# The order of value matmuls and row transposes in a fused attention loop

## The chip, the cores and the metric

One core of a Trainium2 chip. The metric is the device time of one execution in microseconds. The kernel before takes 1733.1 us (median of 3 executions, 1732.15 to 1733.57).

## What is computed

Four layers follow each other on x, 2048 tokens of width 256; each adds a layer-normed result to x. The change concerns the first alone, latent attention:

```
n   = layernorm(x)
cq  = rms_norm(n @ w_qa.T)            # 192 wide
q   = (cq @ w_qb.T), 16 heads of 128 + 64 (the 64 with rotary positions)
ckv = n @ w_kva.T                     # 64 latent + 64 rotary
scores = q k^T * scale, causal; attn = softmax(scores)
out = attn @ v, all heads, @ w_o.T
x   = x + layernorm(out)
```

A mixture of experts, a gated linear recurrence and a quantized feed-forward layer follow. Each of them starts from layernorm(x) and is not touched.

## The kernel before

The kernel runs in stages; each is a block in which the five engines work through queues of their own, tied by semaphores. The first stage (to about 100 us) makes the latents and folds the weights. The second, 100 to 1271 us, is the attention loop in which the change lies. The others (1275 us to the end) do the three later layers.

**Work of the loop.** The 16 tiles of 128 query rows are taken in pairs, a long one and a short one: 15 and 0, 14 and 1, and so on (`tiles_in_order`, L469). A group is 4 heads of one tile, and groups alternate between the long tile and the short one: group 0 is tile 15, group 1 is tile 0, group 2 is tile 15 again; 8 groups to a pair, 64 in all. For each head the key columns up to the diagonal are cut into chunks of up to 4 blocks of 128 keys (`chunk`, L475): 4 chunks a head for tiles 15 to 12 (groups 0 to 31, the long ones), 1 chunk a head for tiles 0 to 3; 3 and 2 chunks in groups 32 to 63. There are 640 chunks. A chunk of n blocks costs n transposes and 3n value matmuls.

**Steps.** TensorE's steps are `project` (the group's queries, L576), `turn` (transposes them, L583, after POOL's rotary steps, L763 to L770, semaphore `roped`), `scores` (L597 to L602), `probs` (transposes the exponentials of a chunk, L615), `values` (L657 to L659, three matmuls a block: the split of the transposed probabilities in `pT_hi` and `pT_lo` times the latents), `o_turn` (L623, transposes normalised head results), `sum` (L641, output projection over all heads of a tile, 24 matmuls) and `x_turn` (L630, transposes the normed rows of the tile for the next layer).

**Transpose banks.** `probs`, `o_turn` and `x_turn` take turns on two PSUM banks, `pT[0]` and `pT[1]`, in the order of the plan (`t_index`, L545). Before the n-th of them TensorE waits in `bank_t` (L604) until ScalarE has copied the one two before it out (L697 `pT_hi`, L702, L706) and VectorE has subtracted (L818 `pT_lo`, L822, L826 `lT_lo`):

```
if n >= 2:
    pe.wait_ge(sem("t_hi"), n - 1)
    pe.wait_ge(sem("t_lo"), n - 1)
return pT[n % 2]
```

**Values and the group's end.** All 4 heads of a group gather in the one bank `pO`. After the last values of a group VectorE takes the reciprocal of the row sums (L834) and writes `O` (L836, `o_out`); the first values of the next group wait for that (L651):

```
if c == 0 and p % HG == 0 and p:
    pe.wait_ge(sem("o_out"), p // HG)
```

In VectorE's queue `o_out` stands at the step of the group's last values, and the `pT_lo` of the probs step just before it comes right behind (L873 to L879).

**The plan.** One list of steps, written by a planner (L481 to L542), sets the order on all engines. Scores of a chunk are appended, and after them, by a small table (L529), `one_behind()` is called 0 to 3 times: it appends `probs(at)`, then `values(at - 2)` (LAG is 2), and then counts down the steps in `later` (`pass_steps`). `later` holds, among others, what follows a tile's sum: `y_measure` after 2 calls, `y_add` after 4, `x_measure` after 5, `x_norm` after 7 and `x_turn` after 8 (L515). `x_norm` (ScalarE, L719) writes `xn` when POOL has the deviation (L141, L143, L777); `x_turn` transposes it; `x_turn` number u belongs to the u-th tile in order. Sixteen of these exist; the last two lie behind the last values. `turn` of a group is planned at the second head of the group before it, and `sum` at the third head of a group. In the plan before, `x_turn` 0, 2 and 4 stand one scores step ahead of a `turn`, with two more calls and then a `sum` behind it; 6, 8, 10 and 12 likewise, with the 3- and 2-chunk tiles; 1, 3 and 5 stand right before the boundary from a short tile into a long one; 7, 9, 11 and 13 stand two scores ahead of the probs of the next long group.

Of the kernel before, what the change touches and what calls it, by code (L numbers as in the profile page):

```python
# [41 lines left out]
HG = 4  # L42
# [32 lines left out]
def build(nc, x, w_lat, w_qn, w_qpe, w_kn, w_v, w_o, q_ln, kv_ln, cos2, sin2, gw, wg, wu, wd, sel,  # L75
          l_in, l_gate, l_b, l_lam, qg, qu, qd, sg, su, sd, out):
    with ExitStack() as whole:
# [89 lines left out]
        with ExitStack() as att:  # L167
# [279 lines left out]
            with ExitStack() as loop:  # L447
# [27 lines left out]
                chunk = [(p, c, min(4, tile_at(p) + 1 - 4 * c)) for p in range(NP) for c in range(tile_at(p) // 4 + 1)]  # L475
                first = [next(n for n, k in enumerate(chunk) if k[0] == p) for p in range(NP)] + [len(chunk)]
                n_chunks = first[NP]
                LAG = 2


                plan = [("project", 0), ("turn", 0), ("project", 1)] + [("scores", k) for k in range(first[1])]  # L481
# [3 lines left out]
                def pass_steps():  # L485
                    for entry in list(later):
                        entry[0] -= 1
                        if entry[0] <= 0:
                            plan.append(entry[1])
                            later.remove(entry)  # L490

                def one_behind():
                    at = state["behind"]
                    plan.append(("probs", at))
                    if at >= LAG:
                        values_planned(at - LAG)
                    state["behind"] += 1
                    pass_steps()

                def values_planned(at):  # L500
                    plan.append(("values", at))
                    p = chunk[at][0]
                    if at + 1 != first[p + 1] or p % HG != HG - 1:
                        return
                    u, g = groups[p // HG]
                    if g == 1:
                        later.append([2, ("o_turn", (u, 0))])
                    if g == 3:
                        later.append([2, ("o_turn", (u, 1))])
                        sums_due.append(u)  # L510

                def sum_heads():
                    u = sums_due.pop(0)
                    plan.append(("sum", u))
                    for delay, step in ((2, "y_measure"), (4, "y_add"), (5, "x_measure"), (7, "x_norm"), (8, "x_turn")):  # L515
                        later.append([delay, (step, u)])

                state = {"behind": 0}
                for p in range(1, NP):
                    n = first[p + 1] - first[p]  # L520
                    placed = False
                    for k in range(n):
                        if k == 0 and p % HG == 2 and sums_due and ("o_turn", (sums_due[0], 1)) in plan:
                            sum_heads()
                        plan.append(("scores", first[p] + k))
                        last = k == n - 1
                        if k == 0 and p % HG == 1 and p // HG + 1 < NG:
                            plan.append(("turn", p // HG + 1))
                        for _ in range({4: (1, 0, 0, 3), 3: (1, 0, 2), 2: (0, 2), 1: (1,)}[n][k]):  # L529
                            one_behind()  # L530
                            if last and not placed:
                                placed = True
                                if p % HG == 3 and p // HG + 2 < NG:
                                    plan.append(("project", p // HG + 2))
                while state["behind"] < n_chunks:
                    one_behind()
                for k in range(LAG):
                    values_planned(n_chunks - LAG + k)
                while later or sums_due:
                    if sums_due and ("o_turn", (sums_due[0], 1)) in plan:  # L540
                        sum_heads()
                    pass_steps()  # L542
# [541 lines left out]
        with ExitStack() as banks:  # L1084
# [70 lines left out]
            plan = [("up", 0), ("up", 1), ("gate", 0), ("split", 0), ("gate", 1)] + [step for slot in slots for step in slot]  # L1155
# [458 lines left out]
```

## Time and profile before

| | |
|---|---|
| median of 3 executions | 1733.1 us |
| the profiled execution | 1734.25 us, its span 1732.5 us |
| mean granted TensorE clock | 0.976 of full speed |
| TensorE matmul busy | 1568.3 us (91% of the span) |
| TensorE weight loads | 1322.7 us (76%) |
| VectorE busy | 1207.4 us (70%) |
| ScalarE busy | 1021.0 us (59%) |
| POOL busy | 301.2 us (17%) |

How to read it: the span is from the first to the last instruction of the profiled execution; the time holds some 1.8 us around it. Busy shares are of the whole span. Matmuls overlap on the array, so two rows that start 0.03 us apart can each be 0.19 us long: for TensorE the distance from start to start tells what a step costs. "Idle before" is the time that an engine did nothing before an instruction, and the name behind the arrow is what ended it.

### The profile page before, as it was taken

The numbers are of one execution on the slowest core, as the hardware profiler recorded it, in microseconds if no ns is written. First come the engines' busy times: TensorE is split into PE (matmuls) and PEld (weight loads), VectorE is DVE, ScalarE is ACT, GpSimd is POOL, SyncE is SP. The second block draws the span as 40 slices with busy tenths as digits, with TensorE's granted clock in tenths as the row PEclk, the third lists the DMA queues.
The fourth block names the chain that finished last, engine by engine and source line by source line (L and its number), as shares of the span: only waits on it lengthen the run. The fifth ranks groups of instructions, "written<-read, shape, count | busy, mean of one in ns | idle before, by whom it ended". The sixth has DMA issues, their size and how long they took to land. (4 is left out here: it accounts for less than half of the span.)

```text
span 1732.5 us, 38201 instructions
## 1 busy us (share of the span) xinstructions
PE 1568.3 (91%) x14452; PEld 1322.7 (76%) x14452; DVE 1207.4 (70%) x2600; ACT 1021.0 (59%) x2017; POOL 301.2 (17%) x743
## 2 busy tenths in 40 slices
PE   3679999999899999999999999999938999988997
PEld 1357787788788778888888888888836878866886
DVE  3847776777777677778777878787855547566564
ACT  2336665666576566667667667667624355555573
POOL 3511111211111211211121121121010012020231
PEclk9879999999999999999999999999978999999999
DMA  8000000000000000000000000000012200000000
GB/s 240 1 0 2 2 1 2 2 2 2 2 1 2 2 1 2 2 2 2 2 2 2 2 2 2 2 2 2 2 40 65 57 1 1 1 28 13 1 25 25
DMA packets 27814, 23.54 MB, mean 14 GB/s; under 512 B 9692, under 2 KB 25180, under 8 KB 27508
## 3 DMA queue, kind: packets, MB, share of 16 engines
q1 hardware_dynamic: 22324, 14.77, 3.1%
q10 hardware_dynamic: 5312, 6.33, 1.2%
q8 instruction: 120, 1.97, 0.5%
q14 instruction: 58, 0.48, 0.1%
HBM read 19.00 MB, written 2.10 MB: 12 GB/s over the span
## 5 line engine op out<-in xcount | busy, mean ns | idle before, releaser
L697 ACT ACTIVATE pT_hi<-pT 128x512 f16<-128x512 f32 (+3 forms) x640 | 341.2, 533 | 304.5 <-PE pT L615 303.0
L818 DVE TENSOR_TENSOR pT_lo<-pT,pT_hi 128x512 f16<-128x512 f32 (+3 forms) x640 | 387.4, 607 | 149.0 <-ACT pT_hi L697 141.9
L686 ACT ACTIVATE pr<-pS,nmx 128x512 f32<-128x512 f32 (+3 forms) x640 | 400.4, 626 | 26.1 <-DVE nmx L809 24.6
L806 DVE TENSOR_REDUCE cmx<-pS 128x1 f32<-128x512 f32 x576 | 338.7, 616 | 65.3 <-PE pS L602 59.9
L615 PE MATMUL pT<-ident,pr 128*128 128x128 f32 x2176 | 347.8, 276 | 16.4 <-DVE pT_lo L818 14.8
L615 PEld LDWEIGHTS pT<-ident,pr 128*128 128x128 f32 x2176 | 252.3, 140 | 48.6 <-ACT pr L686 24.7
L657 PE MATMUL pO<-c_hi,pT_hi 128*128 128x65 f16 x2176 | 265.6, 194 | 18.4 <-DVE O L836 17.7
L597 PE MATMUL pS<-lT_hi,qT_hi 128*128 128x512 f32 (+2 forms) x640 | 265.8, 415 | 3.0 <-ACT pr L686 3.0
L658 PE MATMUL pO<-c_lo,pT_hi 128*128 128x65 f16 x2176 | 266.4, 193 | 0.0
L659 PE MATMUL pO<-c_hi,pT_lo 128*128 128x65 f16 x2176 | 263.7, 192 | 0.0
L602 PE MATMUL pS<-lT_hi,qT_lo 128*128 128x512 f32 (+2 forms) x640 | 256.3, 400 | 0.0
L598 PE MATMUL pS<-lT_lo,qT_hi 128*128 128x512 f32 (+2 forms) x640 | 234.9, 367 | 0.0
L1221 PE MATMUL pGU<-lT_hi,W_all 128*128 128x512 f32 (+1 forms) x640 | 220.4, 403 | 16.0 <-ACT sgb L1301 12.1
L657 PEld LDWEIGHTS pO<-c_hi,pT_hi 128*128 128x128 f16 x2176 | 205.9, 97 | 28.4 <-ACT pT_hi L697 20.5
L658 PEld LDWEIGHTS pO<-c_lo,pT_hi 128*128 128x128 f16 x2176 | 204.1, 98 | 6.6
L659 PEld LDWEIGHTS pO<-c_hi,pT_lo 128*128 128x128 f16 x2176 | 205.2, 97 | 0.0
L1221 PEld LDWEIGHTS pGU<-lT_hi,W_all 128*128 128x128 f32 (+1 forms) x640 | 121.2, 189 | 47.3 <-ACT sgb L1301 16.3
L763 POOL TENSOR_TENSOR qt<-qs,sn 128x128 f32<-128x128 f32 x64 | 29.2, 456 | 704.6 <-ACT qs L674 704.6
L602 PEld LDWEIGHTS pS<-lT_hi,qT_lo 128*128 128x128 f32 x640 | 124.1, 194 | 16.8
L597 PEld LDWEIGHTS pS<-lT_hi,qT_hi 128*128 128x128 f32 x640 | 120.8, 189 | 16.9 <-ACT pr L686 3.0
L598 PEld LDWEIGHTS pS<-lT_lo,qT_hi 128*128 128x128 f32 x640 | 122.1, 191 | 11.2
L1221 PE MATMUL pGU<-lT_lo,W_all 128*128 128x512 f32 (+1 forms) x320 | 127.2, 398 | 0.0
(243 smaller groups left out, 2507.3 us busy)
## 6 DMA issues: line engine op xcount, KB each, us to landing
X<-in_x SPq DMA_DIRECT2D x4, 512.0 KB, 6.9
wo<-in_w_o ACTq DMA_DIRECT2D x1, 2048.0 KB, 14.1
out<-X SPq DMA_DIRECT2D x8, 256.0 KB, 2.0
raw<-in_wd SPq DMA_DIRECT2D x14, 128.0 KB, 2.1
raw<-in_wg SPq DMA_DIRECT2D x13, 128.0 KB, 2.8
raw<-in_wu SPq DMA_DIRECT2D x13, 128.0 KB, 2.7
wqn<-in_w_qn ACTq DMA_DIRECT2D x1, 1536.0 KB, 17.8
raw<-in_qg SPq DMA_DIRECT2D x6, 128.0 KB, 2.5
```

Source lines behind the costliest of these rows:

```text
L597: pe.matmul(o, q_hi, lT_hi[:, 2, ks], start=True, stop=False)
L598: pe.matmul(o, q_hi, lT_lo[:, 2, ks], start=False, stop=False)
L602: pe.matmul(o, q_lo, lT_hi[:, 2, ks], start=False, stop=True).then_inc(sem("scored"), 1)
L615: m = pe.transpose(o[:, k * P:(k + 1) * P], pr[:, at % RING, k * P:(k + 1) * P], ident[:])
L657: pe.matmul(o, hi, c_hi[:, j, 0:KVL + 1], start=(j == 0), stop=False)
L658: pe.matmul(o, hi, c_lo[:, j, 0:KVL + 1], start=False, stop=False)
L659: m = pe.matmul(o, lo, c_hi[:, j, 0:KVL + 1], start=False, stop=(j == tile_at(p)))
L686: act.activation(pr[:, at % RING, 0:n * P], pS[at % 4][:, 0:n * P], ACT.Exp, bias=nmx[:, p % 4:p % 4 + 1]).then_inc(sem("exped"), 1)
L697: act.activation(pT_hi[:, a % 4, 0:chunk[a][2] * P], src, ACT.Copy).then_inc(sem("t_hi"), 1)
L806: ch.inc(dve.tensor_reduce(cmx[:, p % 2, c:c + 1], pS[at % 4][:, 0:n * P], AX.X, ALU.max))
L818: dve.tensor_tensor(pT_lo[:, a % 4, 0:w], src, pT_hi[:, a % 4, 0:w], ALU.subtract).then_inc(sem("t_lo"), 1)
L1221: mm = pe.matmul(pGU[bank % 3][0:r, :], W_all[:, m, 2 * g + i, k * P:k * P + r], xT[j][:, k, ts], start=(q == 0), stop=(q == 5))
```

## The change

In `one_behind`, values are no longer planned at once but put in `values_due`. If the first one due is the first chunk of a group, and no `scores` step stands in the plan since the values before it, it is held until the next call, and then both are planned, behind the next `probs`. All other values are planned in the same call as before. At the end of the plan what is still due comes before the last two. Beside that, `x_turn` comes 10 calls after its sum in place of 8. The instructions of each step and their waits stay as they are; the waits count in the new order.

```diff
--- before.py
+++ after.py
@@ -493,7 +493,13 @@
                     at = state["behind"]
                     plan.append(("probs", at))
                     if at >= LAG:
-                        values_planned(at - LAG)
+                        values_due.append(at - LAG)
+                    new_group = values_due and chunk[values_due[0]][1] == 0 and chunk[values_due[0]][0] % HG == 0
+                    done = ("values", values_due[0] - 1) if values_due else None
+                    drained = not new_group or done not in plan or any(k[0] == "scores" for k in plan[plan.index(done):])
+                    if drained or len(values_due) > 1:
+                        while values_due:
+                            values_planned(values_due.pop(0))
                     state["behind"] += 1
                     pass_steps()
 
@@ -512,10 +518,11 @@
                 def sum_heads():
                     u = sums_due.pop(0)
                     plan.append(("sum", u))
-                    for delay, step in ((2, "y_measure"), (4, "y_add"), (5, "x_measure"), (7, "x_norm"), (8, "x_turn")):
+                    for delay, step in ((2, "y_measure"), (4, "y_add"), (5, "x_measure"), (7, "x_norm"), (10, "x_turn")):
                         later.append([delay, (step, u)])
 
                 state = {"behind": 0}
+                values_due = []
                 for p in range(1, NP):
                     n = first[p + 1] - first[p]
                     placed = False
@@ -534,8 +541,8 @@
                                     plan.append(("project", p // HG + 2))
                 while state["behind"] < n_chunks:
                     one_behind()
-                for k in range(LAG):
-                    values_planned(n_chunks - LAG + k)
+                for at in values_due + list(range(n_chunks - LAG, n_chunks)):
+                    values_planned(at)
                 while later or sums_due:
                     if sums_due and ("o_turn", (sums_due[0], 1)) in plan:
                         sum_heads()
```

## Rows read from the trace of the kernel before

**Rows 1.** Window 100 to 1275 us: length, busy by engine, clock, DMA share, GB/s

```profile
100.00:1275.00 1175.00, 1101.54 (x12017) 953.87 (x12016) 879.05 (x1813) 754.65 (x1490) 200.95 (x484) 0.99 0.01 2
```

**Rows 2.** Groups by line, TensorE: count, busy, mean ns, idle before, releasers

```profile
L615 PE MATMUL pT<-ident,pr 128*128 128x128 f32 x2176 | 347.8, 276 | 16.4 <-DVE pT_lo L818 14.8 <-ACT pr L686 0.4
...
L657 PE MATMUL pO<-c_hi,pT_hi 128*128 128x65 f16 x2176 | 265.6, 194 | 18.4 <-DVE O L836 17.7 <-DVE pT_lo L818 0.5
...
L630 PE MATMUL pT<-ident,xn 128*128 128x128 f32 x32 | 7.3, 314 | 15.4 <-ACT xn L719 13.8 <-ACT pT_hi L697 1.0 <-DVE pT_lo L818 0.6
```

**Rows 3.** Timeline, boundary into group 14: start, length, engine, line [idle before]

```profile
384.82 0.42 DVE L836 TENSOR_TENSOR O<-pO,rl 128x256 f32<-128x256 f32 x1
385.16 0.68 DVE L818 TENSOR_TENSOR pT_lo<-pT,pT_hi 128x512 f16<-128x512 f32 x1
...
385.39 0.19 PE L657 MATMUL pO<-c_hi,pT_hi 128*128 128x65 f16 x1 [0.65 <-DVE O L836]
...
385.66 0.19 PE L657 MATMUL pO<-c_hi,pT_hi 128*128 128x65 f16 x1
...
385.99 0.30 PE L615 MATMUL pT<-ident,pr 128*128 128x128 f32 x1
```

**Rows 4.** Timeline, boundary into group 10, TensorE

```profile
315.72 0.63 PE L615 MATMUL pT<-ident,pr 128*128 128x128 f32 x4 [1.47 <-DVE pT_lo L818]
316.19 0.19 PE L657 MATMUL pO<-c_hi,pT_hi 128*128 128x65 f16 x1
```

**Rows 5.** Timeline, x_turn 0 and the turns after x_turn 0 and 4

```profile
292.21 0.44 PE L630 MATMUL pT<-ident,xn 128*128 128x128 f32 x2 [0.91 <-ACT xn L719]
292.41 0.37 PE L597 MATMUL pS<-lT_hi,qT_hi 128*128 128x256 f32 x1
...
294.67 0.49 PE L583 MATMUL pQ<-ident,qs 128*128 128x128 f32 x3
...
292.99 0.45 POOL L770 TENSOR_TENSOR qs<-qs,qt 128x128 f32<-128x128 f32 x1
...
585.89 0.46 POOL L770 TENSOR_TENSOR qs<-qs,qt 128x128 f32<-128x128 f32 x1
...
587.92 0.60 PE L583 MATMUL pQ<-ident,qs 128*128 128x128 f32 x4
```

**Rows 6.** Timeline, after x_turn 6 and x_turn 12: POOL, TensorE, VectorE

```profile
731.30 0.46 POOL L770 TENSOR_TENSOR qs<-qs,qt 128x128 f32<-128x128 f32 x1
...
731.93 0.61 PE L583 MATMUL pQ<-ident,qs 128*128 128x128 f32 x4
...
734.49 0.36 PE L641 MATMUL pQ<-Wvo_hi,OT_hi 128*128 128x256 f32 x1
...
734.20 0.68 DVE L818 TENSOR_TENSOR pT_lo<-pT,pT_hi 128x512 f16<-128x512 f32 x1
...
1141.64 0.36 PE L641 MATMUL pQ<-Wvo_hi,OT_hi 128*128 128x256 f32 x1
...
1142.01 0.68 DVE L818 TENSOR_TENSOR pT_lo<-pT,pT_hi 128x512 f16<-128x512 f32 x1
```

**Rows 7.** Timeline, around x_turn 9, TensorE then VectorE

```profile
889.21 0.44 PE L630 MATMUL pT<-ident,xn 128*128 128x128 f32 x2 [1.26 <-ACT xn L719]
...
891.68 0.63 PE L615 MATMUL pT<-ident,pr 128*128 128x128 f32 x4
...
892.33 0.47 PE L597 MATMUL pS<-lT_hi,qT_hi 128*128 128x512 f32 x1
...
893.12 0.52 PE L615 MATMUL pT<-ident,pr 128*128 128x128 f32 x3
...
892.29 0.68 DVE L818 TENSOR_TENSOR pT_lo<-pT,pT_hi 128x512 f16<-128x512 f32 x1
...
893.62 0.69 DVE L818 TENSOR_TENSOR pT_lo<-pT,pT_hi 128x512 f16<-128x512 f32 x1
```

**Rows 8.** Timeline, the tail, TensorE

```profile
1267.66 0.69 PE L630 MATMUL pT<-ident,xn 128*128 128x128 f32 x2 [4.33 <-ACT xn L719]
```

## Prediction

> **What bounds the kernel now.** I read the busy times by window first. In the attention loop (100 to 1275 us) TensorE is busy 94% of the time with its clock at 0.99 of full speed, VectorE 75%, ScalarE 64% [rows 1]. TensorE works through its queue in order, so a wait that it removes is time won, and work pushed out of a wait is time lost, unless another wait swallows it. The groups by line show where it idles: 16.4 us before the transposes of the probabilities (14.8 of them until a `pT_lo`), 18.4 us before the values (17.7 until `O`), 15.4 us before the transposes of the normed rows (13.8 until `xn`) [rows 2]. The change aims at the last two. The most that it can win is therefore about 17.7 plus 15.4 less what the tail keeps: `x_turn` 14 alone waits 4.33 us for its rows, with nothing left to put in front of it [rows 8].
>
> **Part one, the first values of a group.** I replayed the planner: 31 of the 63 group boundaries have no scores between the old group's last values and the new group's first, all those in the 4-chunk/1-chunk half (tiles 15 to 12 beside tiles 0 to 3); boundaries in the other half are unchanged. No instruction is added or removed. Call the new group's first chunk d. The order was probs(d+1), values(d-1), probs(d+2), values(d), probs(d+3), values(d+1); it becomes probs(d+1), values(d-1), probs(d+2), probs(d+3), values(d), values(d+1).
>
> What then waits? probs(d+3) writes the transpose bank of probs(d+1), so it waits for `pT_lo`(d+1). VectorE's queue runs `O` of the old group first and that `pT_lo` right behind it. At the boundary into group 14 `O` ends at 385.24 and `pT_lo` at 385.84; the values start at 385.39, 0.15 after `O`, and probs(d+3) at 385.99, 0.15 after `pT_lo` [rows 3]. So the old order already ran probs(d+3) at the first moment its bank was free, and the values lay hidden between two waits that VectorE sets. The new order waits for the later of the two (385.99, as before) and then still has the values to do. Nothing is won; each boundary loses the issue time of values(d). Four blocks of three matmuls start 385.39, 385.66 (the fourth): 0.27 over nine matmuls, 31 ns each, 0.092 us a block [rows 3].
>
> By blocks: the 16 entries into a small tile have 1, 2, 3 or 4 blocks, four entries each, 40 blocks, 3.7 us. The 15 entries into a wide tile have 4 blocks; three of them are in part two, the other 12 give 48 blocks, 4.4 us. Sum 8.1 us. What swallows some: between a small entry and the wide one about 6 us later VectorE is nearly saturated, and where the y and x steps also lie there (three times, 9 blocks, 0.8 us) its own queue sets the next boundary. I take 1.0 off: **plus 7.1**. Bounds: half of it, 3.6, if VectorE swallows the small entries and more; 9 if the switch between kinds of matmul also costs. Below zero is excluded by the pinned bank.
>
> The 31 ns can be set against a rule. "TensorE: Matmul & The Clock Gate", section Back-to-back issue gap, of the Trainium skill gives 81 ns for a pair of weight load and matmul of 128 columns in a real stream; by that figure, as an estimate, the 264 matmuls would cost 21 us. The rows decide here.
>
> **Part two, the normed rows.** `x_turn` moves two probs steps later. It issues two transposes (0.20 us of TensorE: 292.21 to the next at 292.41 [rows 5]), one copy on ScalarE and one subtract on VectorE; no DMA is concerned, POOL's order stays. It uses a transpose bank too, so moving it changes which bank every step between gets. Four kinds of place:
>
> (a) x_turn 0, 2, 4. TensorE idles 0.91 at the first [rows 5]. Once that is gone, the `turn` behind it becomes late: it needs POOL's rope, which ends at 293.44 for a turn at 294.67, and at 586.35 for one at 587.92 [rows 5]; a turn that waits for it starts about 0.15 after (731.76 to 731.93 is the nearest row [rows 6]). So 1.08, 1.08 (the middle one has the same distance as the first) and 1.42 are won. The moved `x_turn` lands ahead of a sum that waits for `qT_lo` anyway. **Minus 3.5.** Bounds 3.0 and 3.9.
>
> (b) x_turn 1, 3, 5, just ahead of a wide entry. It took the bank of probs(d+2), which therefore stood 1.47 us behind `pT_lo` [rows 4]. Now probs(d+2) runs before the wait (0.47 saved, 315.72 to 316.19) and `x_turn` (0.20) after it; values(d) are no longer in a gap but were not before either. **Minus 0.7** for three; 0.5 to 0.9.
>
> (c) x_turn 6, 8, 10, 12. The turn behind it starts 0.17 after the rope [rows 6], so the turn cannot move, and nothing is won. The transposes now come right before the head sum, two banks behind a probs whose `pT_lo` is late: for 6 it ends at 734.88, for 12 at 1142.69, while the sums began at 734.49 and 1141.64 [rows 6]. The sum needs no transpose bank; `x_turn` does. With 0.15 and its own 0.20 the sums start at 735.23 and 1143.04: 0.74 and 1.40 lost; by the same steps 1.07 and 1.22 for 8 and 10. The sum takes 3 us and drains every queue, so this is kept. **Plus 4.4.** Bounds 3.0 (the `pT_lo` comes earlier because `lT_lo` has left its front) and 5.5.
>
> (d) x_turn 7, 9, 11, 13. Taking 9: its 1.26 us go, but probs 421 waits for a `pT_lo` that is tied to `qT_lo`, so TensorE is only 0.83 ahead. `x_turn` then waits for the `pT_lo` of 892.29 to 892.97, 0.41 earlier without the subtract: it starts at 892.70, the scores behind it at 892.90 where they were at 892.33. The transposes at 893.12 then fall into the other bank and need the `pT_lo` of 893.62 to 894.31, less 0.4, behind `O`: 894.05 [rows 7]. With the values, which waited a little before, 0.8 us is lost. The others, whose rows repeat the pattern, give 0.75, 0.6 and 0.5. **Plus 2.6.** Bounds 1.0 and 3.5.
>
> The tail: x_turn 14 now follows the 15th's norm on ScalarE, which waits for its own deviation anyhow; zero.
>
> **Sum.** 7.1 - 3.5 - 0.7 + 4.4 + 2.6 = plus 9.9 us. The profiled execution took 1734.25 (span 1732.5), 1.15 over the median of 1733.1; it would become 1744.2, the median 1743.0. About 0.2% (3.5 us) is what a measurement can tell from no change.
>
> **The rivals.**
> - *Faster.* The moved rows keep all that their stalls cost outside the tail (15.4 less the 4.33 of x_turn 14 and somewhat for the last one, about 10.5), and the displaced values vanish in the next wait. That needs ScalarE and VectorE to run (c) and (d) early enough that the bank is free when `x_turn` comes, 0.75 to 1.4 us earlier than rows 6 show. Point of decision: whether the sum starts before its `pT_lo` plus 0.35. For it: the stalls are real, VectorE is 25% idle. Against: the `pT_lo` hang on the pinned `turn`. 1733.1 - 10.5 = 1722.6, some 1723. Chance 0.08.
> - *No change to be seen.* Half of the values' cost swallowed (3.6), (c) and (d) at their low bounds (4.0), (a) and (b) as above (-4.2): plus 3.4, 1736.5; a little less is 1735. Chance 0.14, with the case that few boundaries are really deferred (then part two alone, plus 2.8).
> - *Slower still.* The copies of the moved rows, now among the densest copies of (d), delay `O` and all behind it, and the switch costs: 9 - 3.5 - 0.5 + 5.5 + 3.5 + some 3 = plus 17, 1750. Chance 0.13.
> - *Forecast.* 1743, own range 1737 to 1748. Chance 0.65.
>
> The range 1736 to 1748 takes the forecast's bounds (3.6 - 3.9 - 0.9 + 3.0 + 1.0 = 2.8 at the lowest, 9 - 3.0 - 0.5 + 5.5 + 3.5 = 14.5 at the highest) and leaves the faster case and most of the slowest outside. Chances: faster 0.08, within 0.2% 0.14, slower 0.78.
>
> **What would show it.** In the profile after: the idle time before the values until `O` is near 0, and about as much and more (some 35 to 40 us: the 16.4, the 17.7 and part of the values' 8.1) stands before the transposes of the probabilities until `pT_lo`; probs(d+3) starts 0.15 after it. The idle time before `x_turn` until `xn` keeps only the tail's; some 2 to 4 us until `pT_lo` take its place. Turns 10, 18 and 26 start 0.15 after the rope. The span from 100 to 715 us grows by about 3, from 715 to 1275 by about 7. The prediction is wrong if probs(d+3) starts without a wait, if the sums 7 to 13 start no later against their turns than now, or if the loop's first half gets shorter.

## The result, and the profile after

The changed kernel takes 1742.56 us (median of 5, 1740.94 to 1747.11) against 1733.1 (median of 5, 1731.09 to 1735.1): plus 9.5 us, a ratio of 1.006 with a 95% interval of 1.005 to 1.0071. The forecast was 1743.0. The profiled execution is the slowest of the five, 1747.11 with a span of 1745.4; what is known of the 4.6 us between it and the median is told at the end. The lines of the code after L518 are 7 higher than before (L615 is now L622, L657 is L664, L630 is L637, L818 is L825, L836 is L843).

First TensorE's groups by line in the changed kernel, with the columns of [rows 2]:

```profile
L622 PE MATMUL pT<-ident,pr 128*128 128x128 f32 x2176 | 347.7, 276 | 32.3 <-ACT pT_hi L704 16.7 <-DVE pT_lo L825 13.7 <-ACT lT_hi L713 0.9
...
L664 PE MATMUL pO<-c_hi,pT_hi 128*128 128x65 f16 x2176 | 262.6, 194 | 0.6 <-DVE pT_lo L825 0.5
...
L590 PE MATMUL pQ<-ident,qs 128*128 128x128 f32 x256 | 39.7, 279 | 7.6 <-POOL qs L777 7.0
...
L630 PE MATMUL pT<-ident,O 128*128 128x128 f32 x128 | 20.1, 280 | 17.6 <-ACT pT_hi L704 15.0 <-DVE pT_lo L825 2.4
L637 PE MATMUL pT<-ident,xn 128*128 128x128 f32 x32 | 7.1, 307 | 11.9 <-DVE pT_lo L825 6.3 <-ACT xn L726 5.2 <-ACT pT_hi L704 0.4
```

Two of these groups in the kernel before, which [rows 2] leave out:

```profile
L583 PE MATMUL pQ<-ident,qs 128*128 128x128 f32 x256 | 39.7, 278 | 4.2 <-POOL qs L770 3.6
...
L623 PE MATMUL pT<-ident,O 128*128 128x128 f32 x128 | 20.1, 280 | 1.4 <-DVE pT_lo L818 0.5
```

The 17.7 us that the values waited for `O` are gone, as the change wants it. They stand elsewhere: the transposes of the probabilities idle 32.3 us where it was 16.4, and the transposes of the heads (`o_turn`, L630, the old L623) idle 17.6 us where it was 1.4. The normed rows' 13.8 us until `xn` have shrunk to 5.2, the tail's alone, but 6.3 us until `pT_lo` stand there now where it was 0.6; and the turns wait 7.0 us for POOL's rope where it was 3.6. The work is the same; the waits have moved and TensorE's order behind them is worse.

Why `o_turn`: replayed, the plan has one between probs(d+2) and probs(d+3) at 15 of the 31 boundaries, those behind the second and the fourth group of a tile. There `o_turn` takes the bank of probs(d+1) and is the step that waits for `pT_lo`(d+1); probs(d+3) follows it, and the held values come behind both. The price is that of the other boundaries, as e1 shows.

The boundary into group 14 again, VectorE, ScalarE, TensorE, to be held against [rows 3]:

```profile
385.98 0.42 DVE L843 TENSOR_TENSOR O<-pO,rl 128x256 f32<-128x256 f32 x1
386.33 1.47 DVE L825 TENSOR_TENSOR pT_lo<-pT,pT_hi 128x512 f16<-128x512 f32 x2
...
385.27 0.60 ACT L704 ACTIVATE pT_hi<-pT 128x512 f16<-128x512 f32 x1 [1.63 <-PE pT L622]
...
387.15 0.52 PE L622 MATMUL pT<-ident,pr 128*128 128x128 f32 x3 [1.26 <-ACT pT_hi L704]
387.51 0.19 PE L664 MATMUL pO<-c_hi,pT_hi 128*128 128x65 f16 x1
...
388.24 0.48 PE L604 MATMUL pS<-lT_hi,qT_hi 128*128 128x512 f32 x1
```

From the start of `O` to the transposes behind it were 385.99 - 384.82 = 1.17 us before and are 387.15 - 385.98 = 1.17 now. TensorE then does the first two chunks of values together, 387.51 to 388.24. The releaser column names ScalarE's `pT_hi`; the one that this bank needs had ended at 385.87. The first of the two subtracts of the L825 row is the one that the step needs: it ends at 387.01 (its length in the kernel before was 0.68), 0.14 ahead of the transposes. Experiment e6 shows it.

Around x_turn 0, to be held against [rows 5]:

```profile
294.58 0.45 POOL L777 TENSOR_TENSOR qs<-qs,qt 128x128 f32<-128x128 f32 x1
...
295.18 0.63 PE L590 MATMUL pQ<-ident,qs 128*128 128x128 f32 x4
...
296.36 0.41 PE L637 MATMUL pT<-ident,xn 128*128 128x128 f32 x2
```

The turn starts 0.15 after the rope's end (295.03); it was 1.23. `x_turn` stands behind it, without a wait. Turn 18 starts 0.15 after the rope too, turn 26 0.24 after it: there the scores ahead of the turn end no sooner, and the rope is not the limit.

Ahead of sums 7 and 13, to be held against [rows 6]:

```profile
735.42 0.63 PE L590 MATMUL pQ<-ident,qs 128*128 128x128 f32 x4 [0.74 <-POOL qs L777]
...
738.54 0.41 PE L637 MATMUL pT<-ident,xn 128*128 128x128 f32 x2 [0.37 <-ACT pT_hi L704]
738.77 0.36 PE L648 MATMUL pQ<-Wvo_hi,OT_hi 128*128 128x256 f32 x1
...
737.71 0.68 DVE L825 TENSOR_TENSOR pT_lo<-pT,pT_hi 128x512 f16<-128x512 f32 x1
...
1151.61 0.41 PE L637 MATMUL pT<-ident,xn 128*128 128x128 f32 x2 [1.01 <-DVE pT_lo L825]
1151.88 0.35 PE L648 MATMUL pQ<-Wvo_hi,OT_hi 128*128 128x256 f32 x1
```

From turn 34 to sum 7 were 734.49 - 731.93 = 2.56 us and are 3.35; the turn itself, with the stall ahead of it gone, waits 0.74 us for the rope. `x_turn` starts 0.15 after the end of `pT_lo` (738.39).

Around x_turn 9, to be held against [rows 7]:

```profile
897.96 0.68 DVE L825 TENSOR_TENSOR pT_lo<-pT,pT_hi 128x512 f16<-128x512 f32 x1
...
899.29 0.69 DVE L825 TENSOR_TENSOR pT_lo<-pT,pT_hi 128x512 f16<-128x512 f32 x1
...
898.79 0.41 PE L637 MATMUL pT<-ident,xn 128*128 128x128 f32 x2 [1.04 <-DVE pT_lo L825]
898.96 0.48 PE L604 MATMUL pS<-lT_hi,qT_hi 128*128 128x512 f32 x1
900.12 0.52 PE L622 MATMUL pT<-ident,pr 128*128 128x128 f32 x3 [0.22 <-ACT lT_hi L713]
```

This is the chain of part (d): `x_turn` behind one `pT_lo`, and the next transposes in the other bank, behind the next `pT_lo` (899.98), 0.14 after it.

**Place by place.** The plan has the same turns and sums in every kernel here, so the timeline gives for each of them by how much it starts later than in the kernel before. What the difference grows by between two of them is what the place between them cost. This table is worked out so, in us, from one profile of each kernel; its first row is how far a kernel is ahead where the loop begins, before anything of its edit:

```
                           forecast       after                e2 (turns alone)
start of the loop             -           -0.57                -4.14 (clock)
held values, all 31          +7.1         +8.4                  -
x_turn 0, 2, 4      (a)      -3.5         -1.06 -1.05 -1.29    -1.04 -1.02 -1.30
x_turn 1, 3, 5      (b)      -0.7         -0.27 -0.30 -0.33    -0.50 -0.49 -0.43
x_turn 6, 8, 10, 12 (c)      +4.4         +0.79 1.10 1.27 1.47 +0.79 1.10 1.27 1.46
x_turn 7, 9, 11, 13 (d)      +2.6         +0.71 0.76 0.61 0.24 +0.71 0.76 0.61 0.25
the loop                     +9.9         +11.0                +2.5
```

### The profile page after: what moved, and what is told of

It reads as the page before. It is cut to its first block and busy times, and to the rows that moved or that the text cites. A ratio compares the mean times of both kernels' runs of the same rounds, so it can differ in the third digit from the quotient of the medians.

```text
span 1745.4 us, 38201 instructions
## 1 busy us (share of the span) xinstructions
PE 1569.1 (90%) x14452; PEld 1322.4 (76%) x14452; DVE 1210.2 (69%) x2600; ACT 1022.2 (59%) x2017; POOL 301.5 (17%) x743
## 5 line engine op out<-in xcount | busy, mean ns | idle before, releaser
L825 DVE TENSOR_TENSOR pT_lo<-pT,pT_hi 128x512 f16<-128x512 f32 (+3 forms) x640 | 387.8, 607 | 146.2 <-ACT pT_hi L704 139.2
L622 PE MATMUL pT<-ident,pr 128*128 128x128 f32 x2176 | 347.7, 276 | 32.3 <-ACT pT_hi L704 16.7
L622 PEld LDWEIGHTS pT<-ident,pr 128*128 128x128 f32 x2176 | 252.4, 140 | 66.8 <-ACT pr L693 43.2
L664 PE MATMUL pO<-c_hi,pT_hi 128*128 128x65 f16 x2176 | 262.6, 194 | 0.6 <-DVE pT_lo L825 0.5
L664 PEld LDWEIGHTS pO<-c_hi,pT_hi 128*128 128x128 f16 x2176 | 205.8, 97 | 4.1 <-ACT pT_hi L704 0.9
L1228 PEld LDWEIGHTS pGU<-lT_hi,W_all 128*128 128x128 f32 (+1 forms) x640 | 121.2, 189 | 47.5 <-ACT sgb L1308 16.4
## 6 DMA issues: line engine op xcount, KB each, us to landing
wo<-in_w_o ACTq DMA_DIRECT2D x1, 2048.0 KB, 13.8
wqn<-in_w_qn ACTq DMA_DIRECT2D x1, 1536.0 KB, 17.7
```

Source lines behind the costliest of these rows:

```text
L622: m = pe.transpose(o[:, k * P:(k + 1) * P], pr[:, at % RING, k * P:(k + 1) * P], ident[:])
L664: pe.matmul(o, hi, c_hi[:, j, 0:KVL + 1], start=(j == 0), stop=False)
L825: dve.tensor_tensor(pT_lo[:, a % 4, 0:w], src, pT_hi[:, a % 4, 0:w], ALU.subtract).then_inc(sem("t_lo"), 1)
L1228: mm = pe.matmul(pGU[bank % 3][0:r, :], W_all[:, m, 2 * g + i, k * P:k * P + r], xT[j][:, k, ts], start=(q == 0), stop=(q == 5))
```

## The experiments

Medians and ratios are against the kernel before, run on the same chip (medians there 1732.0 to 1733.2).

**e1, the held values alone.** The change with its other part undone:

```diff
-                    for delay, step in ((2, "y_measure"), (4, "y_add"), (5, "x_measure"), (7, "x_norm"), (10, "x_turn")):
+                    for delay, step in ((2, "y_measure"), (4, "y_add"), (5, "x_measure"), (7, "x_norm"), (8, "x_turn")):
```

> Only the values part of the change; x_turn stays at 8 steps. Theory (the transposes behind the held values wait for the same pT_lo as before, so the values' issue time is laid bare): 0.37 us at each wide entry, 0.1 to 0.37 at each small one, except at the three boundaries with an x_turn ahead of them, where less; the loop 8 to 9 us longer, 1741 to 1742 us. The idle time before the values until O goes to near 0 and comes back before the transposes. Rival one (the wait is filled, the loss of the whole change is all in the moved x_turn): 1733 or less. Rival two (half is swallowed by VectorE between a small and a wide entry): plus 4 to 5, 1737.5.

Measured: 1740.79 us, ratio 1.005 (1.0036 to 1.0064). The turns put the loop at plus 8.4. The groups by line:

```profile
L622 PE MATMUL pT<-ident,pr 128*128 128x128 f32 x2176 | 347.2, 276 | 30.6 <-DVE pT_lo L825 16.8 <-ACT pT_hi L704 12.7 <-ACT pr L693 0.4
...
L664 PE MATMUL pO<-c_hi,pT_hi 128*128 128x65 f16 x2176 | 262.9, 194 | 0.6 <-DVE pT_lo L825 0.5
```

By place: a wide entry costs 0.36 to 0.41 us (one 0.26), a small one 0.13, 0.19, 0.29 and 0.37 for tiles 0, 1, 2 and 3, so 0.13 for the first block and some 0.08 for each further one; the three wide entries behind an `x_turn` cost 0.00. Entries with an `o_turn` between the two probs cost the same as those without: tile 0 costs 0.12 to 0.13 at both kinds. Both rivals fall: the wait is not filled, and nothing is swallowed between a small and a wide entry.

**e2, the moved x_turn alone.** The kernel before with (10, "x_turn").

> Only x_turn at 10 steps; the values are not held. Theory (each place has its own sign): minus 1.1 to 1.4 us at x_turn 0, 2 and 4; minus 0.3 to 0.7 at 1, 3 and 5; plus 0.8 to 1.5 at 6, 8, 10, 12 just ahead of the sum; plus 0.2 to 0.8 at 7, 9, 11, 13; together plus 1 to 3, 1734 to 1736 us. Rival (the move is a plain gain of its 10 us of stalls, and the loss of the whole change lies in the values alone): 1723 us, and e1 at 1750.

Measured: 1735.86 us, ratio 1.0018 (1.001 to 1.0027); the loop plus 2.5, as in the table. The stalls before `x_turn` did shrink:

```profile
L630 PE MATMUL pT<-ident,xn 128*128 128x128 f32 x32 | 7.1, 307 | 12.0 <-DVE pT_lo L818 6.3 <-ACT xn L719 5.2 <-ACT pT_hi L697 0.4
```

8.6 us of the 13.8 until `xn` are gone, 5.7 of them are back until `pT_lo`, so that the group idles 12.0 us where it was 15.4; and the kernel is slower. The plain-gain rival falls. e1 and e2 add up to the whole change: 8.4 + 2.5 = 10.9 against 11.0 in the loop. At one kind of place they do not: x_turn 1, 3 and 5 win 1.42 us here and 0.90 in the whole change. With `x_turn` out of the way the values have their gap ahead of `O` back (0.66 us of idle time before them at the boundary into group 10 in e2), and holding them lays them bare again; in e1, with `x_turn` still there, it cost nothing.

**e6, held values and pT_lo ahead of O.** e1, and in VectorE's queue, at the first 31 boundaries:

```diff
                             elif step == "values" and at + 1 in first and chunk[at][0] % HG == HG - 1:
+                                if turned is not None and at < 316:
+                                    t_lo(turned)
+                                    turned = None
                                 o_out(chunk[at][0] // HG)
```

> As e1, and at the first 31 boundaries VectorE makes pT_lo ahead of O. Theory (the transposes wait for pT_lo, not for pT_hi as the releaser column says): they start about 0.45 us earlier at a wide entry and 0.2 to 0.4 at a small one, and the values behind them then wait for O, which is later by the pT_lo; the wait is partly filled at last: 0.25 us won at a wide entry, 0.1 at a small one, against e1 minus 4 to 6, some 1737 us. Rival (the transposes wait for ScalarE's pT_hi): they start where they do in e1, O is later by up to 0.6 us, and the time is e1's or more, 1742 to 1750.

Measured: 1741.31 us, ratio 1.0045 (1.0032 to 1.0058). The boundary into group 2, first in e1 and then in e6:

```profile
165.35 0.42 DVE L843 TENSOR_TENSOR O<-pO,rl 128x256 f32<-128x256 f32 x1
165.69 0.68 DVE L825 TENSOR_TENSOR pT_lo<-pT,pT_hi 128x512 f16<-128x512 f32 x1
...
164.61 0.60 ACT L704 ACTIVATE pT_hi<-pT 128x512 f16<-128x512 f32 x1 [1.62 <-PE pT L622]
165.85 0.59 ACT L704 ACTIVATE pT_hi<-pT 128x512 f16<-128x512 f32 x1
...
166.52 0.63 PE L622 MATMUL pT<-ident,pr 128*128 128x128 f32 x4 [1.39 <-ACT pT_hi L704]
166.98 0.19 PE L664 MATMUL pO<-c_hi,pT_hi 128*128 128x65 f16 x1
```

```profile
165.17 0.69 DVE L825 TENSOR_TENSOR pT_lo<-pT,pT_hi 128x512 f16<-128x512 f32 x1
165.98 0.42 DVE L843 TENSOR_TENSOR O<-pO,rl 128x256 f32<-128x256 f32 x1
...
164.53 0.60 ACT L704 ACTIVATE pT_hi<-pT 128x512 f16<-128x512 f32 x1 [1.62 <-PE pT L622]
165.78 0.59 ACT L704 ACTIVATE pT_hi<-pT 128x512 f16<-128x512 f32 x1
...
166.00 0.63 PE L622 MATMUL pT<-ident,pr 128*128 128x128 f32 x4 [0.95 <-ACT pr L693]
166.55 0.19 PE L664 MATMUL pO<-c_hi,pT_hi 128*128 128x65 f16 x1
```

ScalarE's rows are the same to 0.08, `pT_lo` ends 0.51 earlier, and the transposes start 0.52 earlier, 0.14 to 0.15 after it in both: they wait for `pT_lo`, whatever the releaser column names. At this place all that e1 lost is won back (plus 0.02 against the kernel before). Over all boundaries it is 1.0 us in the loop (plus 7.4 against 8.4), not the 4 to 6 that I wrote: at 15 of the 31 boundaries an `o_turn` stands between the two probs, and that needs the `O` which now comes later (its idle time is 18.9 us, 16.7 of it until `O`); and with tiles 2 and 3 the values wait for `O` too. The medians (1741.31 and 1740.79) are too coarse to show it. The mechanism holds, the size was missed.

```profile
L630 PE MATMUL pT<-ident,O 128*128 128x128 f32 x128 | 20.5, 283 | 18.9 <-DVE O L843 16.7 <-ACT pT_hi L704 1.4 <-DVE pT_lo L825 0.5
```

**e7, the same swap in the kernel before.**

> The kernel before, with VectorE's pT_lo ahead of O at the first 31 boundaries; nothing else. Theory: the first values of a group wait 0.2 (tile 0) to 0.6 us longer for O and the transposes behind them come later by the same less what they waited for pT_lo: plus 0.45 to 0.5 at a wide entry, 0.15 to 0.5 at a small one, plus 8 to 13, 1741 to 1746 us. Rival (the order of the two on VectorE does not matter): 1733.

Measured: 1743.07 us, ratio 1.0059 (1.0046 to 1.0071); the loop plus 9.9. The values wait 37.1 us where it was 18.4:

```profile
L657 PE MATMUL pO<-c_hi,pT_hi 128*128 128x65 f16 x2176 | 265.9, 194 | 37.1 <-DVE O L836 27.6 <-ACT pT_hi L697 8.9 <-DVE pT_lo L818 0.5
```

The rival falls. So at a boundary VectorE's two outputs are the bound, and TensorE's order fits VectorE's only if what waits for the first of them comes first.

**e3, x_turn 0 to 5 alone.** `(10 if u < 6 else 8, "x_turn")` in the kernel before.

> The kernel before with x_turn 0 to 5 alone at 10 steps. Theory (each place has its own sign, and the places do not act on each other): minus 1.04, 1.02 and 1.30 at 0, 2 and 4, minus 0.4 to 0.5 each at 1, 3 and 5, as in e2; together minus 4.8, 1728.4 us. Rival (the early moves only shift the work, and what they win is lost again further on): within 1 us of before.

Measured: 1729.33 us, ratio 0.998 (0.9969 to 0.999). Between turn 2 and the last sum the loop is 4.9 us shorter, with -1.06, -1.08, -1.32 and -0.52, -0.50, -0.42 at the six places; beyond x_turn 5 nothing above 0.15. The rival, that the win is lost further on, falls.

**e4, x_turn 6, 8, 10, 12 alone.**

> The kernel before with x_turn 6, 8, 10 and 12 alone at 10 steps. Theory (the moved transposes wait for the bank of two probs before, right ahead of the sum): plus 0.79, 1.10, 1.27 and 1.46 as in e2, plus 4.6, 1737.8 us, nothing anywhere else. Rival (the loss seen there in e2 comes from the earlier moves): within 1 us of before.

Measured: 1739.22 us, ratio 1.0034 (1.0022 to 1.0045), and plus 0.79, 1.10, 1.26 and 1.46 at the four sums. The rival falls; the places do not act on each other. The median is 6.5 us over the kernel before, the loop 4.7: six executions spread from 1734.29 to 1740.95.

**e8, as e3, and x_turn 7, 9, 11, 13 at 11 steps.**

> As e3, and x_turn 7, 9, 11 and 13 at 11 steps: after the values of the next probs, with two scores steps behind them. Theory (what decides is the bank: there the pT_lo it needs is done or nearly so, and 1.5 us of scores give the next bank its time): the stalls of 1.59, 1.26, 0.92 and 0.59 go, 0.2 to 0.4 of each comes back; against e3 minus 1 to 3, 1726.5 us. Rival (any x_turn near the boundary costs what it cost in e2, 0.25 to 0.76 each): plus 2 against e3, 1730.

Measured: 1730.66 us, ratio 0.9987 (0.9978 to 0.9996), and 0.03, 0.19, 0.17 and -0.11 at the four places (the last is -0.15 in e3): nothing won, up to 0.2 lost. Both expectations miss. The transposes behind the boundary, then VectorE:

```profile
746.91 0.48 PE L597 MATMUL pS<-lT_hi,qT_hi 128*128 128x512 f32 x1
748.34 0.52 PE L615 MATMUL pT<-ident,pr 128*128 128x128 f32 x3 [0.48 <-ACT pr L686]
...
747.51 0.68 DVE L818 TENSOR_TENSOR pT_lo<-pT,pT_hi 128x512 f16<-128x512 f32 x1
```

The same transposes and the scores behind them in the kernel before:

```profile
755.29 0.63 PE L615 MATMUL pT<-ident,pr 128*128 128x128 f32 x4
...
756.20 0.48 PE L597 MATMUL pS<-lT_hi,qT_hi 128*128 128x512 f32 x1
```

The stall of 1.59 us is gone, but the lead melts. Counted from turn 35 (748.76 before, 742.37 in e8), the scores right behind the place of the stall start 1.75 us earlier, the transposes of the row above 0.56 earlier, and the next scores (756.20 before, 749.84 in e8) 0.03 later. Those transposes start 0.15 after a `pT_lo` (748.19) which the maxima and `qT_lo` ahead of it in VectorE's queue set: from `turn` 35 on that subtract comes only 0.56 us earlier, and a subtract of 0.42 that belongs to `x_turn` has left its front. So that stall was slack: TensorE waited at `x_turn` for what it would have waited for at the transposes.

**e9, as e8, and for 6, 8, 10, 12 the POOL order changed.**

Of the one line, the last three entries:

```diff
-  (5, "x_measure"), (7, "x_norm"), (8, "x_turn")
+  (6 if late else 5, "x_measure"), (9 if late else 7, "x_norm"), (12 if late else 10 if u < 6 else 11 if u < 14 else 8, "x_turn")
```

with `late = u in (6, 8, 10, 12)`.

> As e8, and for 6, 8, 10 and 12 x_measure at 6 steps (so that POOL ropes the queries before it makes the deviation), x_norm at 9 and x_turn at 12, behind the sum. Theory (these turns stand 0.17 after the rope because the deviation held it up by 1.2 us): the turn comes 0.6 to 0.75 us earlier and the sum with it, minus 0.35 to 0.75 at each place, against e8 minus 2, 1724.5 us. Rival (the turn is held by TensorE's own queue and nothing is won): e8's time, or up to 1 us more for the later transposes.

Measured: 1730.59 us, ratio 0.9986 (0.9977 to 0.9995). The turns come 0.91, 1.09, 1.08 and 0.94 us earlier, more than expected, so they were held by POOL's deviation ahead of the rope. By the next turn 0.99, 0.94, 0.94 and 0.92 are given back: 12 steps put `x_turn` right behind a late `pT_lo` once more. So the turns come as the theory has it, and the 2 us that it wanted against e8 do not.

```profile
732.99 0.41 PE L632 MATMUL pT<-ident,xn 128*128 128x128 f32 x2 [0.63 <-DVE pT_lo L820]
```

**e10, x_turn 0 to 5 at 10, and 6, 8, 10, 12 with their x_turn at 15.** As e9 with `(15 if late else 10 if u < 6 else 8, "x_turn")`.

> e3 (x_turn 0 to 5 at 10 steps), with x_measure at 6, x_norm at 9 and x_turn at 15 steps for 6, 8, 10 and 12, the odd ones from 7 on at 8 as before. In e9 the turn after POOL's ropes came 0.9 to 1.1 us earlier, and the x_turn at 12 gave 0.9 to 1.0 back, with a wait of about 0.6 and transposes of 0.2 right behind the sum. Theory (it is again the bank that decides): at 15 two scores steps follow the x_turn and its bank has long been emptied, so only its 0.2 us come back; 0.7 to 0.9 us at each of the four places stay, minus 3 against e3, some 1726 us. Rival (VectorE and ScalarE swallow it there, as they did at x_turn 7 to 13 in e8): e3's time, 1729 us.

Measured: 1726.23 us, ratio 0.996 (0.9946 to 0.9974), 5.8 us under the kernel before, the fastest of the study. Turns 34, 42, 50 and 58 come 0.90, 1.07, 1.07 and 0.95 us earlier; 0.33, 0.37, 0.34 and, beside the 0.15 that e3 wins there too, 0.34 are given back by the next long group, so 2.6 us stay at the four places. The rival falls. The moved `x_turn` waits for nothing: what the group still idles is the odd ones from 7 on and the tail.

```profile
L632 PE MATMUL pT<-ident,xn 128*128 128x128 f32 x32 | 7.3, 311 | 9.2 <-ACT xn L721 9.0
```

## Why the prediction was right

The mechanism on record is the one that the runs show, with one omission, and its terms can be checked one by one.

- *"The new order waits for the later of the two and then still has the values to do."* Shown by e1 and the boundary into group 14: 1.17 us from `O` to the transposes in both kernels. That the later one is `pT_lo` is shown by e6. What the prediction left out is `o_turn`: at 15 of the 31 boundaries that step, and not probs(d+3), takes the pinned bank, which is why 17.6 us of the waits stand there. It changed the shape of the profile and not the price.
- *Plus 7.1 for the held values.* Mis-sized: 8.4. The sum by blocks, 8.1, was nearly right (a block costs 0.092, and an entry of a single block 0.13). The 1.0 us that I took off for VectorE's full queue was the failing step: in e1 no small entry cost less than its blocks, and the small entries together cost 3.9 for 3.7. The 81 ns of the page "TensorE: Matmul & The Clock Gate", section Back-to-back issue gap, of the Trainium skill are for 128 columns; at 65 columns the trace shows 31 ns, and the sum by the rows held.
- *(a) minus 3.5.* Measured -3.40. Turns 10 and 18 start 0.15 after the rope, as foretold; turn 26 starts 0.24 after it, and its place gave 1.29 for the 1.42 on record.
- *(b) minus 0.7.* Measured -0.90. The step on record (0.47 saved, 0.20 spent) gives 0.27 a place, and the places measure 0.27, 0.30 and 0.33; the 0.7 was rounded below its own working. It missed that the values could have been hidden again there: e2, which does not hold them, wins 1.42.
- *(c) plus 4.4.* Measured +4.63 with 0.79, 1.10, 1.27, 1.47 against 0.74, 1.07, 1.22, 1.40 on record. e4 shows that it stands by itself, e9 that the turn was indeed pinned by POOL.
- *(d) plus 2.6.* Measured +2.32; x_turn 13 was over-priced (0.24 for 0.5), though e1, e3 and e4, which leave that place alone, are 0.14 to 0.15 us shorter there than the kernel before. e8 shows at x_turn 7 what lay under it: the stall was slack behind VectorE. At the other three it is argued from the same result; no place beyond 11 steps was tried there.
- *The foretold shape of the profile.* Between 715 us and the loop's end the loop was to lose 7, and lost 7.0 (plus 3.49 at sum 6, plus 10.45 at the last). Up to 715 us it was to lose 3 and lost 4.1 (from minus 0.57 to plus 3.49); there the held values were mis-sized. The idle time before probs was put at 35 to 40 us; it is 32.3, and the `o_turn` transposes hold another 17.6, which I had not listed apart.

The sum was 9.9; the loop grew by 11.0 and the median by 9.5. That the median came within 0.4 us of the forecast is partly luck: the loop, which the sum is about, missed by 1.1, and the stages around it, which the change does not touch, move a profile by 2 us or more. The rival that ends faster is ruled out by e2, where the stalls until `xn` are gone outside the tail and the loop is 2.5 us longer; the one with no change to be seen by e1, which alone costs 0.5%.

## What to carry to other kernels

Before work is moved into a wait, ask what the work put ahead of it waits for: here it needed the bank whose release came 0.6 us after the one that it was to bridge, so what had been hidden at no cost was laid bare. Steps that rotate through two banks shift the bank of every step behind them when one of them is moved, so each landing place has its own price; read it from the copy two steps before. A place with two scores steps right behind it gave back 0.33 to 0.37 us in e10 of the 0.9 to 1.1 won, but nothing was won at all in e8, where a later wait took it. A stall is only worth its length if no later wait is set by the same engine's queue: in e2, 3.4 us of stalls less before `x_turn` came with 2.5 us more time in the loop.

## What was not expected

- The cost of a moved step repeats from kernel to kernel within 0.05 us where its neighbours are the same, while whole executions spread by 6 us and more (1740.94 to 1747.11 for the change). A few places that an edit leaves alone still differ by 0.12 to 0.15 between profiles.
- In the profiled run of the change 10.45 of its 12.9 us over the kernel before are there at the last sum, after 0.57 gained ahead of the loop, and 2.4 come behind it, in stages that the change doesn't touch. The granted clock is lower there: 0.63 and 0.93 in the 55 us from 1276 and the 70 us from 1551, against 0.66 and 0.95 in the kernel before from 1265 and 1540. That run has the lowest mean clock of the five, 0.974; the others have 0.976 to 0.979 and are 3.9 to 6.2 us shorter. That the clock makes all of that difference is not shown, since the others have no profile.
- Ahead of the edit, too, kernels differ. At turn 0 (112.12 before) e3 is 1.69 us ahead, at turn 2 (149.43) 3.26. Between the two the clock was at 1.2 GHz for less of the stretch, 0.93 against 0.85. First the kernel before, then e3 (window, length, busy by engine, clock):

```profile
112.00:150.00 38.00, 32.27 (x267) 26.36 (x268) 21.92 (x37) 18.77 (x33) 5.22 (x12) 0.85 0.01 1
```

```profile
112.00:150.00 38.00, 32.82 (x313) 27.60 (x314) 24.06 (x42) 20.40 (x38) 5.23 (x12) 0.93 0.00 1
```

- For differences of a few us the turns and sums of one profile say more than the medians: e3's loop is 4.9 us shorter and its median 3.4, e1's 8.4 longer and its median 7.6.
- The engine named as releaser was the wrong one in half of the idle time before the transposes (16.7 of 32.3 us were put down to `pT_hi`), because another `pT_hi` ended within about 0.1 us of the `pT_lo` that counted. A constant distance tells them apart: in all 15 of those waits the transposes start 0.145 to 0.147 us after the end of a `pT_lo`, and 0.00 to 0.10 us after the `pT_hi`. The 13 `o_turn` waits put down to `pT_hi` show the same. Only one of these boundaries was taken apart by an experiment, in e6.
